# Expert slots: the two transposes of a later slot's rows stand in front of the up products instead of behind them

## What is computed

```
normed = layernorm(hidden_states, ln_w, ln_b); xf = normed.reshape(-1, 256)
logits = xf @ router_w                       # 8 experts
top_idx, top_score = argmax(logits), sigmoid(max(logits))
for each expert e:
    xe = xf * where(top_idx == e, top_score, 0)
    routed += (silu(xe @ gate_w[e]) * (xe @ up_w[e])) @ down_w[e]
shared = silu(xf @ sh_gate) * (xf @ sh_up) @ sh_down
x = layernorm(hidden_states + hidden_states + routed + shared)
```

## Time and profile before

| | |
|---|---|
| three runs, median | 1159.86 us |
| the profiled execution's own time | 1158.47 us |
| its span in the trace | 1156.8 us |
| PE busy | 1037.1 us, 90% |
| DVE busy | 700.3 us, 61% |
| ACT busy | 459.7 us, 40% |
| POOL busy | 337.2 us, 29% |
| granted TensorE clock over the span | 0.944 |

### The profile page before, as it was taken

How to read it: one execution, slowest core, us unless ns; L and a number is a source line. 1 busy time by engine, 2 the same in 40 slices (tenths; PEclk the granted TensorE clock), 3 DMA queues, 4 the chain that set the end, 5 groups by cost and what they waited for, 6 DMA issues and landing times. The chain is left out here.

```text
span 1156.8 us, 17516 instructions
## 1 busy us (share of the span) xinstructions
PE 1037.1 (90%) x5522; PEld 541.2 (47%) x5522; DVE 700.3 (61%) x1708; ACT 459.7 (40%) x687; POOL 337.2 (29%) x480
## 2 busy tenths in 40 slices
PE   8991799999999999999982799999994999999995
PEld 4550234444444444444322566666652555555553
DVE  4994688888888888888702455555550233333332
ACT  2442046666666666666670222222220222222221
POOL 2334312222222222222212123333346232222222
PEclk9996579999999999999996699999996999999998
DMA  7557534455554554554009212222112121222121
GB/s 277 140 137 165 80 62 65 68 109 93 88 109 73 102 101 66 102 103 66 11 10 285 57 56 74 75 75 74 38 53 102 56 65 62 67 62 68 61 66 37
DMA packets 78277, 100.06 MB, mean 87 GB/s; under 512 B 28048, under 2 KB 64400, under 8 KB 74864
## 3 DMA queue, kind: packets, MB, share of 16 engines
q1 hardware_dynamic: 67568, 74.41, 31.2%
q0 software_dynamic: 5712, 15.93, 3.7%
q10 hardware_dynamic: 4912, 8.66, 2.3%
HBM read 65.86 MB, written 32.70 MB: 85 GB/s over the span
## 5 line engine op out<-in xcount | busy, mean ns | idle before, releaser
L572 ACT ACTIVATE probs<-scores_ps 128x1024 f32<-128x1024 f32 (+3 forms) x384 | 290.3, 809 | 133.2 <-PE scores_ps L505 131.7
L632 DVE TENSOR_REDUCE maxima<-max_ps 128x1 f32<-128x512 f32 (+2 forms) x352 | 231.6, 687 | 53.0 <-PE max_ps L485 29.2
L481 PE MATMUL max_ps<-k_stack,q_stack 96*128 96x512 bf16 (+3 forms) x768 | 232.9, 345 | 33.5 <-DMA q_stack<-q_parts 32.5
L505 PE MATMUL scores_ps<-q_stack,k_stack 99*128 99x512 bf16 (+3 forms) x768 | 183.0, 328 | 2.2 <-ACT probs L572 2.0
L722 POOL TENSOR_SCALAR_AFFINE_SELECT probs<-probs 128x512 f32<-128x512 f32 x128 | 81.2, 634 | 333.1 <-ACT probs L572 332.2
L525 PE MATMUL out_ps<-probs,v_ones 128*32 128x512 f32 (+3 forms) x1536 | 164.3, 499 | 2.6 <-POOL probs L722 1.8
L481 PEld LDWEIGHTS max_ps<-k_stack,q_stack 96*128 96x128 bf16 x768 | 75.8, 99 | 192.4 <-DVE maxima L628 59.0
L628 DVE CUSTOM_DVE_ANT_0 masked_out<-max_ps,mask_wide 128x384 bf16<-128x384 f32 (+1 forms) x256 | 151.3, 622 | 19.0 <-PE max_ps L481 16.4
L1133 ACT ACTIVATE silu<-gate_ps 128x512 f32<-128x512 f32 x71 | 42.4, 597 | 236.7 <-PE gate_ps L1031 140.0
L505 PEld LDWEIGHTS scores_ps<-q_stack,k_stack 99*128 99x128 bf16 x768 | 69.4, 99 | 53.2 <-ACT probs L572 11.8
L1285 DVE TENSOR_TENSOR hidden<-silu,up_ps 128x512 f32<-128x512 f32 x39 | 26.8, 688 | 104.9 <-PE up_ps L1041 104.9
(11 more groups left out here) (150 smaller groups left out, 1264.2 us busy)
## 6 DMA issues: line engine op xcount, KB each, us to landing
k_stack<-k_parts SPq DMA_DIRECT2D x96, 128.0 KB, 4.5
q_stack<-q_parts SPq DMA_DIRECT2D x96, 128.0 KB, 7.5
q_parts<-parts SPq DMA_DIRECT2D x32, 192.0 KB, 3.2
k_parts<-parts SPq DMA_DIRECT2D x32, 192.0 KB, 3.0
rows_in<-expert_rows SPq DMA_DIRECT2D x39, 136.0 KB
sums_in<-expert_sums SPq DMA_DIRECT2D x39, 128.0 KB, 2.0
x_t<-in_x_cols SPq DMA_DIRECT2D x8, 512.0 KB, 10.9
heads_rows<-heads_out SPq DMA_DIRECT2D x32, 128.0 KB, 1.7
```

Of the source, the lines that this page charges most:

```text
L481: last = nc.tensor.matmul(part, q_stack[:ROWS, u.slot, h0 + k, t * P:(t + 1) * P], k_stack[:ROWS, u.slot, h0 + k, chunk * BLOCK:chunk * BL ...
L505: last = nc.tensor.matmul(scores_ps[:, pair, k, n0:], k_stack[:ROWS_MAX, u.slot, h, mt * P:(mt + 1) * P], q_stack[:ROWS_MAX, u.slot, h, c ...
L572: nc.scalar.activation(probs[:, s % RING, 2 * pair:2 * pair + 2, n0:], scores_ps[:, pair, :, n0:], ACT.Exp).then_inc(exp_done, 1)
L632: nc.vector.tensor_reduce(maxima[:, u.slot, chunk, h0:h0 + heads, t], bank("piece", u.i, n)[:, :heads * keys].rearrange("p (h k) -> p h k" ...
```

## The change

In PE's list of the slot loop the call `turn_rows(j + 2)` moves up by one place, ahead of `expert_up(j + 1)`. Nothing is added or removed, and no other engine's list changes.

```
             for j in range(SLOTS):
                 expert_gate(j + 1)
                 turn_hidden(j)
+                turn_rows(j + 2)
                 expert_up(j + 1)
-                turn_rows(j + 2)
                 expert_down(j)
```

## The result

The changed kernel takes 1222.53 us, the median of four runs (1220.11 to 1224.94), against 1159.36 us before, there too the median of four. The ratio is 1.0541, 95% interval 1.0514 to 1.0568: 63 us slower, where 1221 was forecast. The profiled execution takes 1222.42 us with a span of 1220.7, 63.9 above the one before.

A forecast was written before the change was run, and what follows sets the result against it. The rows' loop, not PE, was taken to bound each pass: 0.87 + 1.82 + 1.92 + 3.47 = 8.08 us against 6.37, over 36 passes 61 us more, giving 1221 us; range 1209 to 1240 for 8 in 10.

The forecast's parts named there:

- the loop of the rows: Slot loop: rows' transfer, PE's transposes and products, `add_sum`, token numbers, next transfer; said to set each pass, 6.37 us before.
- Release to the up products, 0.87: Slot loop, PE: from the rows' release through two transposes and a `value_load` to the up products, 0.87 us.
- Up products 1.82, down products 1.92: Slot loop, PE: up products 1.82 us with first load uncovered, then down products 1.92 us to `add_sum`.
- `add_sum` to the next release, 3.47: Slot loop: from `add_sum` through token numbers and the rows' transfer to its release, 3.47 us, unchanged by the move.
- that unknown (0 to 11 us): Slot loop: cost of the output's scatter overlapping the rows' transfer by 0.7 us; 0 to 11 us in all, taken as 0.
- the 8.08 forecast: Slot loop: the pass after the change, 8.08 us against 6.37, so 1.71 more in each of 36 passes.
- One step in the range: Forecast's range: a delay near 0.7 us between release and up products was said to take 4 us off the total.
- The clock: Rival, slot loop: PE's clock falls in new 1.5 us gaps, 2 us lost a pass; 1293 us, half the passes 1257; chance 0.08.
- the likeliest case: The forecast itself, chance 0.80: 1221 us, range 1212 to 1235, passes about 8.1 us, clock at 1.00 throughout.
- The smaller delay: Rival, slot loop: only 0.4 us from release to up products, 1.24 us more a pass, 1205 us; chance 0.07.
- Rows in time: Rival, slot loop: rows released by the end of hidden's transposes, pass 5.82 us, 20 us saved, 1140 us; chance 0.03.
- the move does nothing: Rival, PE's list: hardware brings the up products' weight loads past the waiting transposes, 1160 us; chance 0.02.

The follow-up runs named there:

- the free extra product: Kernel before plus one unread product per pass, ahead of the wait for the rows (1159.97 us) or beside the `value_load` behind their transposes (1159.27 us).
- all four opened versions: Four row buffers instead of three: 1138.74 us changed order, 1140.15 order of before; token numbers read ahead of `times_up`, three buffers: 1141.26 changed order, 1138.22 order of before.
- the last run: Kernel before plus one unread product in each of passes 1 to 36, behind the `value_load` and waits of the down products: 1168.58 us, ratio 1.0080.

## Why the prediction was right

The mechanism was right. The time was met more closely than the terms deserve, and that is luck: the loop was put 6 us too long, the falls of the clock, 9 us, were left out of the sum, and the two errors nearly cancel.

- *The pass is bound by the loop of the rows, not by PE*: shown, by four buffers, by early token numbers in both orders, and by the free extra product. The 20 us that the loop cost before were real too: 1159 less 20 is what all four opened versions take.
- *Release to the up products, 0.87*: measured 0.75, the mean of 36. This term was too high by 0.12. It was taken from the down products, which have one wait more in PE's list. Whether that wait is the 0.12 stays open. The extra product of the last run stood behind both waits and still started at 0.75; but it takes no address from a register. The up products take one, have a single wait and start at 0.75 too. Down products have both waits and the address, 0.87, and so have the gate products where the rows are turned first, 0.88 on average. No run separates the two.
- *Up products 1.82, down products 1.92*: measured 1.82 and 1.92.
- *`add_sum` to the next release, 3.47*: 3.43 on average. The transfer takes 2.13 from issue to release, as before, though the scatter of the output now reaches into it by some 0.8 us (an estimate: it starts at 1010.30 in the pass shown and its median landing is 2.5 later, the transfer goes out at 1011.95); that unknown (0 to 11 us) was nothing. The 0.04 gained lie between the token numbers and the issue, 0.95 instead of 1.00.
- The terms measured give 0.75 + 1.82 + 1.92 + 3.43 = 7.92 against the 8.08 forecast: 36 x 1.55 = 56 us, not 61. One step in the range was also off: a delay of 0.7 instead of 0.87 makes 36 x 0.17 = 6 us, not 4.
- *The clock*: the likeliest case had it at 1.00 throughout, and that was wrong in 5 passes of 35. The rival had the place and the price (about 2 us a fall; 1.7 measured), but it was taken as all passes or half of them. It brought the missing 8 us. In the changed kernel, with gaps of 1.2 to 1.6 us, 5 of 35 passes had a fall; with the transposes first and gaps of 3.3 to 3.9 every pass had one. The Trainium skill, page "TensorE: Matmul & The Clock Gate", section "HAM oscillation — how this bites in real kernels", tells of a kernel in which every burst behind a DMA wait starts cold. The order with the transposes first agrees with that; the changed kernel, with a fall in five passes only, doesn't.
- *The smaller delay* (0.4, 1205 us) was not the case, but 0.12 of its 0.47 was.
- *Rows in time* and *the move does nothing*: excluded by 36 waits for the transfer of 1.55 us each, and by weight loads of the up products that never came less than 0.73 behind the release.

What the experiments point to, 1138 to 1141 us, comes from either remedy and in either order of the list; the four intervals overlap. In three of the four traces every pass from slot 1 to slot 36 takes 5.82 us; in the fourth, the changed order with early token numbers, two take 6.96 and 6.42, the first with a wait of 0.6 for the rows.

## What to carry to other kernels

When an engine's list holds a wait for a transfer, ask what the transfer itself waits for. If that is the engine's own later product, wait and product are one loop, and a product moved behind the wait costs its length, less what a register load behind the same wait hides (the up products cost 1.55 of their 1.72 us, hidden's transposes 0.11 of their 0.44), while those ahead of it are free up to the loop's slack, even on an engine that looks 95% busy (PE before the change: 213.0 of the 223 us from 911 to 1134). Look first at what releases the buffer: here a 0.14 us copy of token numbers, read behind `add_sum` instead of ahead of `times_up`, was worth 20 us in the order of before and 81 in the changed one.

## What was not expected of the hardware

- Gaps of 1.2 to 1.6 us with one of 0.3 behind them went with a fall of the clock in 5 of 35 passes, and the longest of them was not among the five; seven gaps of 1.02 to 1.04 us in the shared part brought none. In the fall shown above the clock was still 1.00 through the gap itself and fell about 1 us after the up products had begun, so the gap and the slow products lie apart in the trace.
- Unread products that filled the gap bought back 8 us.
